# A decoder layer in one kernel: FFN rows and rope in PSUM, normalising on ScalarE, first pair turned on TensorE

## The reference

```python
# attention: 16 heads of 16, 4 key/value heads
q, k = rms_norm(x Wq + bq), rms_norm(x Wk + bk);  v = x Wv + bv
q, k = rope(q) * gain, rope(k)
a = softmax(causal(q k / 4)) v
x = layernorm(x + a Wo + bo)
# a running weighted mean over time, k = x, v = ctx
y_t = (state_num + exp(u + k_t) v_t) / (state_den + exp(u + k_t));  state = exp(-exp(decay)) * state + exp(k_t) (v_t, 1)
x = layernorm(x + y)
# FFN with weights reduced to their signs, 256 -> 1024 -> 256
h = relu((x sign(Wu)) * up_scale)
x = layernorm(x + (h sign(Wd)) * down_scale * output_scale)
```

## Time and profile before

| | us |
|---|---|
| median of 3 runs | 213.67 |
| lowest and highest | 212.53, 214.04 |
| the profiled execution | 212.72 |
| its span, first to last instruction | 210.9 |
| DVE, PE, ACT, POOL busy in the span | 188.3, 161.2, 130.1, 102.7 |
| mean granted TensorE clock | 0.933 of full speed |

### The profile page before, as it was taken

One profiled execution on the slowest core, in us unless ns is written; L12 is line 12 of the kernel. 1 busy time (PEld: TensorE's weight loads), 2 busy tenths in 40 slices (PEclk: granted clock), 3 DMA queues, 4 the chain that ended last, 5 costly groups with the idle time before them and its releaser, 6 DMA issues.

```text
span 210.9 us, 3915 instructions
## 1 busy us (share of the span) xinstructions
PE 161.2 (76%) x1368; PEld 110.4 (52%) x1368; DVE 188.3 (89%) x390; ACT 130.1 (62%) x246; POOL 102.7 (49%) x115
## 2 busy tenths in 40 slices
PE   1990098998979799699947996975739959699940
PEld 0540053643455465256633785863537838588820
DVE  2679967879998999999999999999987999999992
ACT  1754778569737647968975881588214665649800
POOL 6132200012023347213596779478976698951731
PEclk9997579999999999999999999999676988999995
DMA  6698356072050351510530010100100002001112
GB/s 214 207 406 286 77 59 143 1 145 83 2 97 30 99 84 45 123 54 0 36 93 0 3 50 0 54 2 0 50 0 0 3 0 99 0 8 46 69 37 103
DMA packets 19052, 14.80 MB, mean 70 GB/s; under 512 B 14164, under 2 KB 14420, under 8 KB 18775
## 3 DMA queue, kind: packets, MB, share of 16 engines
q1 hardware_dynamic: 18448, 14.43, 25.0%
q10 hardware_dynamic: 582, 0.10, 0.3%
HBM read 9.28 MB, written 2.10 MB: 54 GB/s over the span
## 4 chain that ended last, share of the span: by engine, by line
PE 40%; DVE 27%; issue 9%; ACT 8%; POOL 7%; DMA 5%; SPq 2%; POOLq 0%; DVEq 0%; ACTq 0%
PE banks L534 7%; PE banks L376 7%; PE banks L443 6%; PE banks L475 5%; DVE x L1514 4%; PE banks L518 3%; DVE ratio L1535 3%; DMA osc_b<-out_s_dram 3%; PE banks L415 3%; ACT probs L880 3%; POOL rstd L1221 3%; ACT hid L927 2%; DMA rows<-stack 2%; DVE hid_lo L1578 2%; DVE ratio L1552 2%
## 5 line engine op out<-in xcount | busy, mean ns | idle before, releaser
L534 PE MATMUL banks<-dn_sb,hid_hi 128*128 128x256 bf16 x128 | 34.2, 303 | 7.8 <-POOL hid_lo L1247 5.2
L880 ACT ACTIVATE probs<-banks 128x1024 f32<-128x1024 f32 x32 | 31.3, 1025 | 10.8 <-PE banks L422 10.8
L1247 POOL TENSOR_TENSOR hid_lo<-hid,hid_hi 128x512 f16<-128x512 f32 x25 | 34.4, 1394 | 3.8 <-ACT hid_hi L933 3.8
L534 PE MATMUL banks<-dn_sb,hid_lo 128*128 128x256 bf16 x128 | 34.2, 303 | 0.0
L927 ACT ACTIVATE hid<-banks,ups_man 128x256 f32<-128x256 f32 x64 | 26.4, 476 | 12.4 <-PE banks L518 12.3
L1218 POOL TENSOR_SCALAR veps<-mv 128x2 f32<-128x2 f32 x24 | 9.6, 402 | 49.3 <-DVE mv L1506 48.3
L518 PE MATMUL banks<-x2hi,up_sb 128*128 128x256 f16 x128 | 28.9, 273 | 3.0 <-DVE x2lo L1571 2.9
L518 PE MATMUL banks<-x2lo,up_sb 128*128 128x256 f16 x128 | 28.9, 272 | 0.0
L376 PE MATMUL banks<-wqkv_sb,xT_sb 128*128 128x384 f32 x64 | 24.7, 533 | 4.7 <-DMA wqkv_sb<-wqkv_dram 4.5
L933 ACT ACTIVATE hid_hi<-hid 128x512 f16<-128x512 f32 x32 | 19.7, 637 | 6.0 <-PE banks L534 5.4
L415 PE MATMUL banks<-rows 32*128 32x512 f16 x128 | 10.7, 409 | 14.6 <-DMA rows<-stack 11.9
(11 more groups left out here) (108 smaller groups left out, 357.7 us busy)
## 6 DMA issues: line engine op xcount, KB each, us to landing
xT_sb<-xT_dram SPq DMA_DIRECT2D x8, 256.0 KB, 4.5
x_sb<-x_dram SPq DMA_DIRECT2D x8, 256.0 KB, 4.0
ctxT_sb<-ctxT_dram SPq DMA_DIRECT2D x8, 256.0 KB, 2.6
out_dram<-outb SPq DMA_DIRECT2D x8, 256.0 KB, 2.0
hid<-up_dram SPq DMA_DIRECT2D x1, 1024.0 KB, 8.5
hid<-down_dram SPq DMA_DIRECT2D x1, 1024.0 KB, 10.6
wqkv_sb<-wqkv_dram SPq DMA_DIRECT2D x1, 384.0 KB, 3.2
wo_sb<-wo_dram SPq DMA_DIRECT2D x1, 256.0 KB, 5.2
```

Source lines behind the costliest of these rows:

```text
L534: mm = nc.tensor.matmul(banks[:, DN[p], t * D:(t + 1) * D], part[:, j, t * S:(t + 1) * S], dn_sb[:, j, :], start=(j == 0 and t == 0 and m ...
L880: nc.scalar.activation(probs[:, (T * p + t) % PROBS_N, 2 * h:2 * h + 2].rearrange("p n j s -> p n (j s)"), banks[:, b:b + 2], ACT.Exp).the ...
L1247: nc.gpsimd.tensor_tensor(hid_lo[:, 2 * n:2 * n + 2], hid[:, p % HID_N, 2 * n:2 * n + 2], hid_hi[:, 2 * n:2 * n + 2], ALU.subtract).then_i ...
```

## The change

- **FFN rows.** `relu` writes its piece back to the PSUM bank from which it reads, for three of four pieces of each pair (n = 0, 1, 3); `high_bits` and `low_bits` read it there. Piece 2 still goes to `hid`. GpSimd does not read PSUM here, so `low_bits` is now 28 times on DVE (24 from PSUM, 4 from `hid`) and 4 times on POOL. The up and down weights get buffers of their own.
- **Rope.** The sines are taken first, to SBUF; the product with cosines is written in place in PSUM; the sum reads PSUM and `rope_b`.
- **Normalising** moves to ACT: `normed` for n = 0 and 1 of all pairs and n = 2 of pairs 0 to 2 (38 of 48 instructions), as `Identity` with scale `rstd` and bias `offset`. POOL makes `offset` = -mean x rstd, two more instructions of one column after each root (38 in all).
- **First pair.** Its 12 blocks of `stack` are transposed on PE into two banks read as f16; ACT copies 8 blocks and DVE 4 into `rows`. The other pairs keep the transposing DMA.
- **Zero products.** PE runs 8 products of a 128x512 tile of zeros, set by POOL, before it waits for the first weights.
- **Who does what.** `num_by_rec` 7 times on POOL, `den_by_rec` once on DVE, `low_heads` 4 times on POOL, `high_heads` 3 times on POOL, `swap_keys` 6 times on ACT, one more `scale_heads` on DVE. The last pair's scaling stays in PSUM.
- **Start.** One bias load to 97 partitions for the projection and one for the output, each split by itself; rope tables and identity are loaded by SP; ACT does the first values and squares before `decay_rates`; DVE does `small_constants` later.
- **Orders and banks** are written anew on every engine.

```diff
-            hid = sb("hid", [128, HID_N, NJ, T * S])
+            hid = sb("hid", [128, HID_N, 2, T * S])
+        IN_SBUF = ((0, 0, 1, 0), (0, 0, 1, 0), (0, 0, 1, 0), (0, 0, 1, 0),
+                   (0, 0, 1, 0), (0, 0, 1, 0), (0, 0, 1, 0), (0, 0, 1, 0))
-        PJ = (0, 2, 4, 4, 6, 6, 6, 4)
+        PJ = (0, 2, 4, 6, 6, 0, 6, 4)
...
+        def hidden(p, n):
+
+            if IN_SBUF[p][n]:
+                return hid[:, sum(IN_SBUF[q][n] for q in range(p)) % HID_N]
+            return banks[:, UP[p][n]].rearrange("p (j s) -> p j s", j=2)
...
+            def first_rows():
+
+                done(pe, "stack_done", 0)
+                pe.wait_ge(ident_half, 1)
+                for b in range(BLOCKS):
+                    mm = nc.tensor.transpose(first_bank[:, b * 128:(b + 1) * 128],
+                                             stack[:, 0, b].rearrange("p g r d -> p (g r d)"), id_h[:])
+                mm.then_inc(first_tr, 1)
...
+            pe.wait_ge(idle_ready, 1)
+            for k in range(WARM):
+                nc.tensor.matmul(banks[:, PJ[0]], idle[:, 0:128], idle[:], start=True, stop=True)
...
+            def normed(n, p):
+
+                done(act, f"rs{n + 1}", p)
+                act.wait_ge(sems[f"of{n + 1}"], T * sum(OFFSETS[n][:p + 1]))
...
+                for t in range(T):
+                    nc.scalar.activation(to[:, t], rows_of[:, t, :], ACT.Identity, bias=offset[n][:, p % MV_N, t:t + 1],
+                                         scale=rstd[n][:, p % MV_N, t:t + 1]).then_inc(signal(name, p), 1)
...
+                if OFFSETS[n][p]:
+                    done(pool, f"rs{n + 1}", p)
+                    for t in range(T):
+                        nc.gpsimd.tensor_scalar(offset[n][:, p % MV_N, t:t + 1], mv[n][:, p % MV_N, t, 0:1],
+                                                rstd[n][:, p % MV_N, t:t + 1], -1.0, ALU.mult, ALU.mult)\
...
+            def rope_cosines(p):
+
+                done(dve, "sin_done", p)
+                q = banks[:, PJ[p]:PJ[p] + T, 0:QK].rearrange("p t (h d) -> p t h d", d=HD)
+                nc.vector.tensor_tensor(q, q, cos_sb[:].unsqueeze(1).unsqueeze(1).to_broadcast([128, T, NQK, HD]), ALU.mult)\
...
-                nc.vector.tensor_tensor(hid_lo[:, 2 * n:2 * n + 2], hid[:, p % HID_N, 2 * n:2 * n + 2],
+                nc.vector.tensor_tensor(hid_lo[:, 2 * n:2 * n + 2], hidden(p, n),
```

More of the change, by code:

```diff
@@ L143, in build @@
         rstd = [sb(f"rstd{n}", [128, MV_N, T]) for n in range(3)]
+        offset = [sb(f"offset{n}", [128, MV_N, T]) for n in range(3)]
         ke = sb("ke", [128, KE_N, NC, 2, T, SEG])
@@ L674, in from_scores @@
                 scores(7, 0, guarded)
-                done(pe, "hid_done", 0)
+                done(pe, "probs_done", 6)
                 mixed_to_tokens(2)
+                products(6, 1)
+                done(pe, "probs_done", 7, 1)
+                ffn_up(0, 3)
+                done(pe, "z_done", 2)
+                x2_to_channels(1)
+                ffn_down(0, 2)
+                done(pe, "att_done", 6, 1)
+                x1_to_channels(4)
+                products(7, 0)
+                attention_to_tokens(6, 1)
@@ L925, in relu @@
                     act.wait_ge(small_ready, SMALL)
-                for j in (2 * n, 2 * n + 1):
-                    nc.scalar.activation(hid[:, p % HID_N, j, :], banks[:, UP[p][n], (j % 2) * T * S:(j % 2 + 1) * T * S],
+                for s in range(2):
+                    j = 2 * n + s
+                    nc.scalar.activation(hidden(p, n)[:, s], banks[:, UP[p][n], s * T * S:(s + 1) * T * S],
                                          ACT.Relu, scale=ups_man[:, j:j + 1]).then_inc(sems["hid_done"], 1)
@@ L1031, in _ @@
+            take_products(6, 0)
+            take_channels(4)
+            keys(3)
+            relu(0, 0)
+            log_den(2)
+            high_bits(0, 0)
+            first_rec(2)
+            done(act, "wo_mm", 4)
+            take_channels(5)
+            normed(1, 1)
+            relu(0, 1)
+            act.wait_ge(dn_ready, NJ)
+            relu(0, 2)
+            high_bits(0, 1)
+            high_bits(0, 2)
             exps(6, 1, 0)
-            take_channels(5)
-            take_products(6, 0)
@@ L1452, in rope_sum, with first_rows_out @@
                 done(dve, "sin_done", p)
-                nc.vector.tensor_tensor(rot[:, p % ROPE_N], rot[:, p % ROPE_N], rope_b[:, p % ROPE_N], ALU.add)\
-                    .then_inc(signal("rot_done", p), 1)
+                nc.vector.tensor_tensor(rot[:, p % ROT_N].rearrange("p (t h) d -> p t (h d)", t=T),
+                                        banks[:, PJ[p]:PJ[p] + T, 0:QK],
+                                        rope_b[:, p % ROPE_N].rearrange("p (t h) d -> p t (h d)", t=T), ALU.add)\
+                    .then_inc(sems["rot_done"], 1)
+            def first_rows_out():
+                dve.wait_ge(first_tr, 1)
+                half = 8
+                nc.vector.tensor_copy(rows[:, 0, half:BLOCKS].rearrange("p b s -> p (b s)"),
+                                      first_bank[:, half * 128:BLOCKS * 128]).then_inc(first_out, 1)
             def scale_heads(p):
@@ L1547, in keys_by_context, with den_by_rec @@
                     .then_inc(signal("kv_done", p), 1)
+            def den_by_rec(p):
+                done(dve, "rec0_done", p)
+                nc.vector.tensor_tensor(newt[:], ratio[:, :, 1], rec0[:], ALU.mult).then_inc(signal("newt_done", p), 1)
             def num_by_rec(p):
@@ L1773, in _ @@
             done(dve, "ny_done", 4)
             mix(5)
-            add_mixed(4)
+            add_out(0)
+            low_bits(2, 0)
+            moments(2, 0)
+            scale_out(1)
+            den_by_rec(5)
+            add_mixed(4)
+            attend_norm(7, 1)
+            low_x2(3)
+            refine(5)
+            low_bits(2, 1)
+            moments(1, 4)
             moments(2, 1)
-            done(dve, "z_done", 4)
-            normed(0, 6)
+            scan(6)
+            low_bits(2, 3)
@@ L1821, in _ @@
+            low_x2(6)
+            low_bits(5, 3)
+            add_mixed(7)
+            moments(1, 7)
             landed(dve, "stored", 1)
```

1108 lines of the change are left out of this document (573 added, 535 removed).

## The result

The changed kernel takes 214.88 us (median of 20 runs, 213.82 to 216.13), the kernel before 213.41 in the same sessions (20 runs). The ratio is 1.0073, 95% interval 1.0049 to 1.0097: the same to 1%, if anything a little slower. I had said 195 us. In the profiled execution the span is 212.4 us (time 214.84).

A forecast was written before the change was run, and what follows sets the result against it. DVE (VectorE), 93% busy from first scores to last product, was taken to set the pace; 212.72 - 5.0 (start) - 12 (middle) = 195.7, given as 195 us; main case 190 to 202, wider range 187 to 205.

The forecast's parts named there:

- start term: Start of the kernel: first scores at 21.0 us instead of 25.95, so -5.0 us, ends -2 and -6.
- middle term: First scores to last product: the 178 us become 146 / 0.88 = 166, so -12 us.
- The 88%: Middle: assumed busy share of TensorE, the longest engine at 146 us, against 93% for the longest engine before.
- The transposes: First pair: 12 added on TensorE, priced at 3.3 us at the low clock and 1.7 at the high one.
- DVE's sum: DVE's busy time over the kernel: 188.3 - 21.8 - 1.5 = 165 us.
- relief by GpSimd: DVE instructions stretched by GpSimd get shorter as GpSimd's work falls: 1.5 us taken, bounds 0 to 6.
- under 162: Sign of being right: TensorE's busy time stays under 162 us.
- near 2.8 us: Start: with zero products ahead, the first eight projection products take near 2.8 us; before, 4.83.
- rival 4: Start: zeros do nothing for the clock, first eight products still 4.8 us; +1 to 2 us, 197; inside the 0.64 main case.
- Rival 2: Middle: normalised rows late on ScalarE, each of 8 pairs holding TensorE 1 to 1.5 us longer; 204 to 208 us; chance 0.13.
- Rival 3: Middle: FFN rows hold their PSUM banks 1.3 us longer in each of 24 pieces and TensorE waits; 227 us; chance 0.03.
- no clock step in the middle: Sign of being right: TensorE's half-clock piece, at 150 to 162 us before, does not recur in the middle.

The follow-up runs named there:

- e1_rows: The changed kernel with the biases loaded as before, three single-row loads into a zeroed buffer: 196.92 us, ratio 0.9243 to the kernel before.
- e2_96and1: The changed kernel with each 97-partition bias load cut into one for 96 partitions and one for the last: 199.31 us, ratio 0.9312 to the kernel before.
- e3_before97: The kernel before, with its three single-row bias loads replaced by one load to 97 partitions: 226.31 us, ratio 1.0623.
- e4_split_later: The changed kernel, both slow bias loads kept, DVE's split of the out biases moved behind the copy of the first pair's rows: 207.52 us, ratio 0.9714.
- e7: e1_rows with 16 more zero products behind the third projection and 4 behind the first pair's transposes: 197.54 us, ratio 0.9262 to the kernel before.
- e5: e1_rows without the zero products: 198.07 us, ratio 0.9293 to the kernel before.
- e9: e1_rows with 8 more subtractions on DVE, one per pair, into a buffer nobody reads: 198.95 us, ratio 0.9321 to the kernel before.
- e11: e1_rows with each pair's second FFN up piece multiplied twice on TensorE, 64 more matmuls: 199.33 us, ratio 0.9354 to the kernel before.

## Why the prediction was wrong

- **The step that failed is the start term**: "Scores at 21.0 instead of 25.95: -5.0 us (ends: -2, if the clock and the early DMAs disappoint, and -6)". It came to +13.6. I priced three DMA issues less on ScalarE (the trace has four less, three for seven) and never the two loads that replaced the single rows, though the diff shows them and their wait ahead of `head_sums(0)` in DVE's order. e1_rows, e2_96and1 and e3_before97 show that price from three sides, e4_split_later the queue's part of it. With the bias as before, the term is 22.33 - 25.95 = -3.6, within its own ends.
- **The middle term, -12, was right**: -12.1 in the changed kernel, -13.2 in e1_rows. Together, 212.72 - 3.6 - 12 = 197.1 against 196.92 measured for e1_rows, so the rest of the sum stands. Its working holds too. From the first scores to the last product, e1_rows has:

```profile
22.33:187.00 164.67, 146.43 (x1338) 101.75 (x1338) 141.81 (x301) 135.25 (x267) 89.68 (x120) 0.97 0.20 49
```

  TensorE is the longest with 146.4 us (146 to 150 predicted) and busy 89% of the stretch (88% taken), DVE has 141.8 (144) and ScalarE 135.3 (137). The 88% was a choice and not derived; that it came out so near is in part luck.
- The transposes were priced too high: 12 of them took 1.46 us at the low clock and 0.84 at the high one (e7), not 3.3 and 1.7. The row behind the price was of f32, and these are f16. Whether transposes bring up the clock stays open: where they ran at the low clock, TensorE had idled 3.1 to 12 us before them.
- DVE's sum: 165 expected, 162.86 measured. `hid_lo` from PSUM took 0.680 us, the 0.682 of the earlier trace rows. The relief by GpSimd was undersized: mixing went from 1.013 to 0.744 us, 16 x 0.27 = 4.3 us, where I took 1.5 for everything (bounds 0 to 6). The rope product in PSUM cost nothing, as taken.
- ScalarE: 151 expected, 146.65 measured, although one normalising took 0.59 to 0.60 us and not 0.50. By group columns ScalarE rose by some 22 us; its busy time rose by 16.5, since overlapping pieces count once there. GpSimd's `offset` took 0.344, not 0.25, 12.5 us in all and not 9.5; that its total of 100.5 is the predicted 2 us less is partly luck, since its other instructions made that up.
- TensorE: "under 162" was wrong for the changed kernel (167.55, with a granted clock of 0.53 from 26 to 45 us), right for e1_rows (161.56).
- Zeros: "near 2.8 us" for the first eight products failed (5.46) behind late weights and a gap; with none it came to 2.82 to 3.99. Their worth, 1.1 us in e5 and inside the noise, does not contradict the 1 to 2 us of rival 4.
- Rival 2 came once, not in each pair. TensorE waited 0.7 and 0.8 us for `x` itself, and 3.14 us for an exponential that stood behind one in ScalarE's queue:

```profile
102.92 2.30 DVE L1697 TENSOR_TENSOR_SCAN state<-dec_sb,ke 128x1032 f32<-128x1032 f32 x1
103.04 2.48 POOL L1368 TENSOR_SCALAR offset<-mv,rstd 128x1 f32<-128x1 f32 x2
...
105.61 1.09 ACT L1021 ACTIVATE x<-z,offset,rstd 128x256 f32<-128x256 f32 x2 [2.35 <-POOL offset L1368]
...
106.61 1.91 ACT L957 ACTIVATE probs<-banks 128x1024 f32<-128x1024 f32 x2
...
107.67 0.66 PE L556 MATMUL banks<-id_f,x 128*128 128x128 f32 x4 [3.14 <-ACT probs L957]
```

- Rival 3 did not come: no wait on FFN banks took its place. That the additions of e9 and e11 come back in part fits the reading that three loads lie close and none bounds alone.
- The clock: "no clock step in the middle" held mostly (0.97 from 45 to 150 us); the step is in the start.

## What to carry to other kernels

Every load that a diff touches has a price of its own, above all those first in the program: read what it was and what it is now, in partitions, packets and who waits, before summing engines. A load to 97 partitions landed some 10 us later here than the same cut in 96 and 1; by the rule cited under e2_96and1 the prime count is why. A load that must be late should not have its wait stand ahead of work that is ready on an in-order queue. Splitting a span at the first scores told at once that one half had won 12 us and the other lost them.

## What was not expected of the hardware

- Two broadcasts of 1.5 and 1 KB to 97 partitions were usable only 14.0 and 23.9 us after their issues; one of 2.5 KB took 18.0 (0.71 to 18.72). The first of them cut in 96 and 1 was there within 4.5 us, the second before DVE came to it at 8.10. From first packet to last these loads took 12.5, 10.6 and 16.1 us, that is 129, 109 and 166 ns per partition.
- While the slow load ran, other loads were late: `wqkv_sb` landed 6.4 us after its issue instead of 3.6 (e1_rows), `gain_in` 14.0 instead of 4.6, and in e3_before97 an issue on the same queue took 3.01 us.
- Short GpSimd instructions took longer while DVE's scan ran (2.3 us): two `offset` took 2.48 us there, 0.50 in most other places, and one `rstd` 2.57 us instead of 0.70.
- The granted clock fell to 0.50 in 20 to 24 us of e1_rows, where TensorE had idled 4.5 us, and stayed at 1.00 there with 20 zero products in the gaps (e7_gap_zeros); the time did not change.
- `Identity` with a scale and a bias per partition, 128x256 from SBUF, takes 0.59 to 0.60 us; the relu of the same size takes 0.462 from and to PSUM and 0.480 from PSUM to SBUF.
